# Graph attention on one core: the adjacency mask kept as -1 and the step function as 127 or infinity

## What is computed

```python
seq    = (x @ W_seq).reshape(N, H, DH)              # N = 2048, D = 512, H = 16, DH = 32
score1 = einsum('nhd,d->hn', seq, a1)
score2 = einsum('nhd,d->hn', seq, a2)
scores = leaky_relu(score1[:, :, None] + score2[:, None, :], 0.2)
attn   = softmax(scores + (1 - adj) * -65500, axis=-1)
hidden = einsum('hij,jhd->ihd', attn, seq).reshape(N, D)
x      = layernorm(x + elu(hidden @ W_out + b_out))
# second layer: dinv = (1 + row sums of (adj + adj.T) / 2) ** -0.5
x      = layernorm(x + adj @ (dinv * (((adj + adj.T) / 2 + I) @ (dinv * x))))
```

## Time and profile before

| what | value |
|---|---|
| median of 3 executions | 741.42 us (740.29 to 742.1) |
| profiled execution, its own time | 740.72 us |
| its span in the trace | 738.9 us |
| granted TensorE clock, mean | 0.998 of full speed |
| busy: PE, DVE, ACT, POOL | 98%, 71%, 55%, 16% of the span |
| prologue, up to the first attention matmul | about 67.6 us |
| attention stage | 67.6 to 447 us |
| all after it | 447 to 738.9 us |

### The profile page before, as it was taken

One profiled execution on the slowest core, in us unless ns is written; L12 is line 12 of the kernel. 1 busy time (PEld: TensorE's weight loads), 2 busy tenths in 40 slices (PEclk: granted clock), 3 DMA queues, 4 the chain that ended last, 5 costly groups with the idle time before them and its releaser, 6 DMA issues.

```text
span 738.9 us, 23474 instructions
## 1 busy us (share of the span) xinstructions
PE 722.7 (98%) x10731; PEld 560.0 (76%) x10731; DVE 526.6 (71%) x885; ACT 409.6 (55%) x315; POOL 117.6 (16%) x145
## 2 busy tenths in 40 slices
PE   7999899999999999999999999999999999999996
PEld 5878899999999999999999995444444444444444
DVE  4568999999999999999999984877830110332332
ACT  1678998888988998898988952333220110000000
POOL 0200110001221212213000002655312100000000
PEclk9999999999999999999999999999999999999999
DMA  9994315213532344333221122994059500101101
GB/s 334 417 419 162 110 54 149 61 46 74 88 63 64 61 82 83 63 65 59 59 59 36 47 82 50 184 188 101 23 87 170 85 1 1 41 31 43 43 29 43
DMA packets 33351, 71.24 MB, mean 96 GB/s; under 512 B 3044, under 2 KB 14052, under 8 KB 31076
## 3 DMA queue, kind: packets, MB, share of 16 engines
q1 hardware_dynamic: 24736, 51.64, 20.3%
q0 software_dynamic: 8240, 17.84, 17.0%
q10 hardware_dynamic: 276, 0.26, 0.1%
HBM read 77.86 MB, written 8.65 MB: 117 GB/s over the span
## 4 chain that ended last, share of the span: by engine, by line
PE 81%; DVE 8%; issue 5%; DMA 4%; SPq 1%; POOL 1%; ACT 0%; POOLq 0%; DVEq 0%; ACTq 0%
PE bank L635 20%; PE bank L742 14%; PE bank L636 12%; PE bank L728 11%; PE bank L691 8%; PE bank L641 4%; PE bank L699 4%; PE bank L640 4%; PE bank L639 4%; DVE RZ L1081 3%; DMA RZ<-in_L_gnn_W_seq_dram 2%; DVE RG L1095 1%; DMA RZ<-s_rows_dram 1%; DVE RG L1091 1%; SPq L345 1%
## 5 line engine op out<-in xcount | busy, mean ns | idle before, releaser
L635 PE MATMUL bank<-RP,RG 128*128 128x132 f16 (+1 forms) x3072 | 375.3, 220 | 2.8 <-DVE RG L1091 1.5
L636 PE MATMUL bank<-RP,MT 128*128 128x66 f16 (+1 forms) x3072 | 375.0, 196 | 0.0
L820 ACT ACTIVATE RZ<-RZ,TAB 128x2048 int8<-128x2048 f32 x159 | 305.0, 1994 | 24.8 <-DVE RG L1091 22.1
L635 PEld LDWEIGHTS bank<-RP,RG 128*128 128x128 fp8e4 x3072 | 284.8, 98 | 3.7 <-DVE RG L1091 1.8
L636 PEld LDWEIGHTS bank<-RP,MT 128*128 128x128 fp8e4 x3072 | 284.7, 97 | 0.0
L640 PE MATMUL bank<-RP,RG 128*128 128x66 f16 (+1 forms) x1024 | 199.2, 194 | 0.0
L641 PE MATMUL bank<-RP,MT 128*128 128x66 f16 (+1 forms) x1024 | 198.9, 194 | 0.0
L639 PE MATMUL bank<-RP,RG 128*128 128x66 f16 (+1 forms) x1024 | 198.0, 193 | 0.0
L1081 DVE TENSOR_SCALAR RZ<-RZ,TAB 128x2048 int8<-128x2048 f32 x97 | 123.0, 1268 | 2.3 <-DMA RZ<-s_rows_dram 2.2
L742 PE MATMUL bank<-RZ,MT 128*128 128x512 f16 (+1 forms) x544 | 110.8, 366 | 0.0
L1091 DVE TENSOR_TENSOR RG<-RZ,MT 128x512 int32<-128x512 int32 x159 | 107.7, 677 | 0.0
(11 more groups left out here) (138 smaller groups left out, 724.1 us busy)
## 6 DMA issues: line engine op xcount, KB each, us to landing
RG<-in_adj_t_dram SPq DMA_DIRECT2D x16, 1024.0 KB, 8.1
RZ<-s_rows_dram SPq DMA_DIRECT2D x60, 256.0 KB, 3.3
seq_copy_dram<-SEQ SPq DMA_DIRECT2D x8, 528.0 KB, 5.4
RZ<-in_x_dram SPq DMA_DIRECT2D x16, 256.0 KB, 3.0
RP<-in_adj_p_dram POOLq DMA_DIRECT2D x8, 512.0 KB, 8.2
RP<-in_adj_tp_dram POOLq DMA_DIRECT2D x8, 512.0 KB, 12.4
out_dram<-W SPq DMA_DIRECT2D x16, 256.0 KB, 2.0
RQ<-in_x_t_dram SPq DMA_DIRECT2D x2, 1024.0 KB, 14.3
```

The costliest lines, as they stand in the source:

```text
L635: mm(bank[:, c:c + 4 * d], step, both, start=(j == 0 and i % IB == 0), **ends)
L636: last = mm(bank[:, c:c + 4 * d].rearrange("p (e c d) -> p e c d", e=2, c=2)[:, :, 1, :], mask, pn[:, 4:6, :], start=False, **ends)
L820: A(Z[:, m % NZ, :], S1B[u], ACT.Sign, bias=S2[:, h, j:j + 1], scale=-1.0).then_inc(z_ready, 1)
```

## The change

The mask MT is kept as -1 in float8 (the cast gets the scale -1). A raw step is the byte 127 on DVE, and on ACT infinity in float8, from a rectifier whose argument is s1 + s2 times 2^40; a new table SK holds S2 times 2^40. Both bytes, anded with the byte of -1, give the byte of +1. So G is +1 as before, and the mask product is now negative. The operands are four slots: high E, high F, low E, low F. The step product takes all four; the mask product takes slots 1 and 3, two runs of 33 with 33 between, and gives G F minus adj F. The final sum becomes a difference. The negation L1009 goes. Slots 0 and 1 are written by ACT, slots 2 and 3 by DVE, each as one run of 66 per tile. The operands of a tile take 264 bytes a partition and not 396, so that TN, TB, ND, V2 and VMT move down in RP. Where the mask is used elsewhere, signs follow (degrees, column sums, -1/ZS at the end).

```diff
-        Z = RZ[:, 0:2048].bitcast(i8).rearrange("p (s n) -> p s n", s=NZ)
+        Z8 = RZ[:, 0:2048].bitcast(f8).rearrange("p (s n) -> p s n", s=NZ)
...
-        PNW = NT * 6 * (DV + 1) // 2
+        PNW = NT * 4 * (DV + 1) // 2
...
-            return RP[:, o:o + NT * 3 * w].bitcast(f16).rearrange("p (t c d) -> p t c d", t=NT, c=6)
+            return RP[:, o:o + NT * 2 * w].bitcast(f16).rearrange("p (t c d) -> p t c d", t=NT, c=4)
...
+                own.mark(gp.tensor_scalar(SK[:, hs], S2[:, hs], STEEP, 1.0, ALU.mult, ALU.mult))
                 own.mark(gp.tensor_scalar(S2[:, hs], S2[:, hs], -1.0, 1.0, ALU.mult, ALU.mult))
...
-                    high, low, edge = (pn[:, c:c + 2, :].rearrange("p c d -> p (c d)") for c in (0, 2, 4))
-                    both = pn[:, 0:4, :].rearrange("p c d -> p (c d)")
+                    high, low = (pn[:, c:c + 2, :].rearrange("p c d -> p (c d)") for c in (0, 2))
+                    both, edge = pn.rearrange("p c d -> p (c d)"), pn[:, 1:4:2, :]
...
-                                      pn[:, 4:6, :], start=False, **ends)
+                                      edge, start=False, **ends)
...
-                            last = mm(bank[:, c + d:c + 3 * d], mask, edge, start=False, **ends)
+                            last = mm(bank[:, c + d:c + 3 * d].rearrange("p (c d) -> p c d", c=2), mask, edge, start=False, **ends)
...
-                A(MT8[:, t, :], adj_f[:, t % NA, :], ACT.Copy, saturate=False, accum_out=CS[:, t:t + 1]).then_inc(adj_cast, 1)
+                A(MT8[:, t, :], adj_f[:, t % NA, :], ACT.Copy, scale=-1.0, saturate=False, accum_out=CS[:, t:t + 1]).then_inc(adj_cast, 1)
...
-                A(operands(h)[:, :, 0:5:4, 0:DV], V2[:, :, :, :], ACT.Copy).then_inc(hi_ready, 1)
+                A(operands(h)[:, :, 0:2, 0:DV], V2[:, :, :, :], ACT.Copy).then_inc(hi_ready, 1)
...
-                A(Z[:, m % NZ, :], S1B[u], ACT.Sign, bias=S2[:, h, j:j + 1], scale=-1.0).then_inc(z_ready, 1)
+                A(Z8[:, m % NZ, :], S1B[u], ACT.Relu, bias=SK[:, h, j:j + 1], scale=STEEP, saturate=False).then_inc(z_ready, 1)
...
+                    own.mark(V.tensor_scalar(half(e, SK), half(e, S2), STEEP, None, ALU.mult))
                     own.mark(V.tensor_scalar(half(e, S2), half(e, S2), -1.0, None, ALU.mult))
...
-                    own.mark(V.memset(pn[:, :, 4, DV], 1.0))
-                own.mark(V.tensor_tensor(pn[:, :, 2:6:3, 0:DV], V2[:, :, :, :], pn[:, :, 0:5:4, 0:DV], ALU.subtract))
-                own.wait(ve)
-                V.tensor_scalar(pn[:, :, 1:4:2, 0:DV], pn[:, :, 4:6, 0:DV], -1.0, None, ALU.mult).then_inc(pn_ready, 1)
+                    own.mark(V.memset(pn[:, :, 0:2, DV], 1.0))
+                    own.wait(ve)
+                V.tensor_tensor(pn[:, :, 2:4, 0:DV], V2[:, :, :, :], pn[:, :, 0:2, 0:DV], ALU.subtract).then_inc(pn_ready, 1)
...
-                at = (DV + 1) + DV
-                V.tensor_copy(r[:, :, 0:IB - 1], wide(h, 0)[:, :, :, at]).then_inc(row_sb, 1)
-                V.tensor_copy(r[:, :, IB - 1], narrow(h, 1, 2)[:, :, DV]).then_inc(row_sb, 1)
+                ones_e, ones_f = DV, (DV + 1) + DV
+                own.mark(V.tensor_copy(r[:, :, 0:IB - 1], wide(h, 0)[:, :, :, ones_e]))
+                own.mark(V.tensor_copy(r[:, :, IB - 1], narrow(h, 0, 1)[:, :, DV]))
+                own.wait(ve)
+                V.tensor_tensor(r[:, :, 0:IB - 1], r[:, :, 0:IB - 1], wide(h, 0)[:, :, :, ones_f], ALU.subtract).then_inc(row_sb, 1)
+                V.tensor_tensor(r[:, :, IB - 1], r[:, :, IB - 1], narrow(h, 1, 2)[:, :, DV], ALU.subtract).then_inc(row_sb, 1)
...
-                own.mark(V.scalar_tensor_tensor(ND, TN[:, :, 0, :], TINY, ND, ALU.add, ALU.add))
+                own.mark(V.scalar_tensor_tensor(ND, TN[:, :, 0, :], TINY, ND, ALU.add, ALU.subtract))
...
-                V.tensor_scalar(ZD[:, m % 2, :], S1B[u], S2[:, h, j:j + 1], -1.0, ALU.is_gt, ALU.mult).then_inc(zd_ready, 1)
+                V.tensor_scalar(ZD[:, m % 2, :], S1B[u], S2[:, h, j:j + 1], STEP, ALU.is_gt, ALU.mult).then_inc(zd_ready, 1)
```

More of the change, by code:

```diff
@@ L37, in gat_then_normalised_adjacency @@
     TINY = 1e-30
+    STEP = 127.0
+    STEEP = 2.0 ** 40
     TOP = 2.0 ** 15
@@ L154, in gat_then_normalised_adjacency @@
         ones = sb("ones", [P, P], bf16)
-        TAB = sb("TAB", [P, 5, H, NT], f32)
-        S1, S2, EE, FF, RHO = (TAB[:, i] for i in range(5))
+        TAB = sb("TAB", [P, 6, H, NT], f32)
+        S1, S2, EE, FF, RHO, SK = (TAB[:, i] for i in range(6))
         VC = sb("VC", [P, 3, H], f32)
@@ L1036, in lone_nodes @@
                 own.mark(V.tensor_scalar(LONE[:, :], ROW[:, :], 0.0, None, ALU.is_equal))
-                own.mark(V.tensor_tensor(DINV[:, :], ROW[:, :], CS[:, :], ALU.add))
+                own.mark(V.tensor_tensor(DINV[:, :], ROW[:, :], CS[:, :], ALU.subtract))
                 own.wait(ve)
@@ L1289, in sum_tile @@
                     ve.wait_ge(out_st[u], (t // 2) * 16)
-                V.scalar_tensor_tensor(yw[:, u, :], pb[(t + NQ) % 8][:, :], 1.0 / ZS, X1[:, t, 0:D],
+                V.scalar_tensor_tensor(yw[:, u, :], pb[(t + NQ) % 8][:, :], -1.0 / ZS, X1[:, t, 0:D],
                                        ALU.mult, ALU.add).then_inc(ov_done, 1)
@@ L1301, in last_half @@
                     ve.wait_ge(out_st[u], (t // 2) * 16)
-                V.scalar_tensor_tensor(yw[:, u, cols], pb[(t + NQ + e) % 8][:, cols], 1.0 / ZS, X1[:, t, cols],
+                V.scalar_tensor_tensor(yw[:, u, cols], pb[(t + NQ + e) % 8][:, cols], -1.0 / ZS, X1[:, t, cols],
                                        ALU.mult, ALU.add).then_inc(ov_done, 1)
```

## The result

| | before | changed |
|---|---|---|
| median | 741.76 us (4 runs) | 734.08 us (4 runs) |
| ratio | | 0.9897 (0.9877 to 0.9916) |
| profiled execution, span | 740.72, 738.9 us | 734.38, 732.6 us |
| matmuls between 90 and 400 us | 7614 | 7742 |

The forecast was 742.7 us with a chance of 0.14 for faster. The time is within about 1 us of the rival called faster, 735.1. The clock did nothing: granted 1.00 in both in the stretch from 90 to 400 us.

What follows compares the result with a forecast made beforehand. PE was taken to bound the attention stage, DVE only its start and a gap in head 7. Terms -0.4 - 0.3 + 2.0 = +1.3 us gave 742.7 us, own range 740.5 to 744, low end 735, high end 753.

Steps and rivals of the forecast that it cites:

- the rival called faster: PE's edge matmuls all cost as the aligned one: -5.6 us, with -0.7 from DVE, 735.1 us; chance 0.14.
- What bounds the kernel: Attention stage: PE sets the pace, DVE barely keeps up and bounds only the stage's start and a head 7 gap.
- The negation, 0.5 us a head: DVE's L1009, once a head: removal frees 8 us over 16 heads, off the path wherever PE sets the pace.
- The start: Chain over DVE before tile 5 of head 0: without L1009 everything behind it moves up, -0.4 us.
- The gap in head 7, -0.3: PE's wait for a late mask, 254.66 to 255.01 us: vanishes as DVE gets ahead, -0.3 us.
- Does a start address matter, +2.0 us: PE's edge matmuls: a start on 16 bytes saves 1.9 ns; none stays aligned, so 68 tiles lose 0.03 us each.
- The break in the run, 0: Edge operand read as two runs of 66 bytes: taken as 0, upper end 102 us at half read speed.
- Both slower rivals: Edge operands: second run costs as off-16-byte start, 750.5 us, chance 0.24; paired reading lost, 755 to 845 us, chance 0.12.
- Steps, table, cast, SK, degrees: 0: Steps on ACT and DVE, ACT table loads, adjacency cast, table SK, head 3's degree subtractions: no added time, 0.

## Why the prediction was wrong

- **What bounds the kernel**: right that PE sets the pace where DVE keeps up, and that DVE barely does. I did not put a number on "barely". Had I taken DVE's heads as I took PE's tiles, I would have found 23.5 against 23.43 us.
- **The negation, 0.5 us a head**: its size was right (DVE's plain heads 23.23 to 22.76). Its worth was mis-stated, because I had it as hidden work wherever PE sets the pace. Left out alone, from head 3 on, it took away the waits in head 7 (that head of PE fell from 23.86 to 23.43 us), and the time fell by 0.3 to 1.8 us (740.38 against 741.07). But with PE's operands moved it is worth 4 to 7 us: 739.91 to 735.78, and 740.87 to 734.08 or 734.58.
- **The start**: tile 5 of head 0 began at 77.81 instead of 78.07 us although the S1 row landed 0.20 us later (61.61), so -0.46, near the -0.4 forecast. The first matmul did not come earlier, 67.72 after 67.63.
- **The gap in head 7, -0.3**: came in part. PE lost 0.32 us before tile 13 and 0.10 before tile 12, which I had overlooked; now it loses 0.20 before tile 13. PE became as much faster as DVE, so DVE's masks were hardly further ahead (0.47 us at the head's start, 0.26 before).
- **Does a start address matter, +2.0 us**: this is the step that failed. The rows' period of four was real and so was its link to 16 bytes. The reason I gave (a start off 16 bytes costs) was wrong, and the trace could not tell it from the right one: in the fast tiles the edge starts on 16 bytes and, being adjacent, the slots end there too. From the wrong one it followed that no edge would be fast; from the right one that all are. The term measured (360.0 - 366.1) x 1024 groups = -6.2 us instead of +2.0. The faster rival had these 1.9 ns an edge and the sign, and no mechanism; it got the least chance but one for that. That its 735.1 came so near is in part luck: it added -5.6 for PE and -0.7 for DVE as if each could be had alone, and PE's part alone gave 1.0 us.
- **The break in the run, 0**: right. Edges of two runs take 30.0 ns, and the run with the edge cut at bytes 264 and 344 shows no cost of the cut. Both slower rivals fall with it. The Trainium skill (Advanced Engine Details and Errata, section "SBUF Cachelines") says that an access to a different line of 16 bytes is penalised, and that two hits on a line are enough to avoid it. No run here shows such a penalty for one line more: the edge touches ten lines now for nine and is faster. That does not refute the section, as all of these lines are read for two or more numbers, save one of the ten in every second tile. The size of the line agrees with the period in the trace.
- **Steps, table, cast, SK, degrees: 0**: right. ACT's step takes 1.994 us as rectifier into eight-bit float as it did as sign into int8, with one table load, and PE waits for no mask in heads 1 to 6, so nothing of the rest reached it. The Trainium skill (ScalarE: Activation LUTs, section "Table sets: the hidden batching unit"), by which a rectifier needs no other set, is borne out by that load.

## What to carry to other kernels

When two engines are both busy 99% of a stage, work out each one's time per repetition from its own starts. If the two agree, as here, a saving on either may be worth next to nothing until the other has one too, and the experiment is the two-by-two of both. And when a period in the trace fits an address rule, list what else has that period (here the end of the read before, as well as the start of this one) before the rule is carried over to a new layout.

## What the runs showed of the hardware that I had not expected

A matmul of 66 columns behind one of 132 starts its successor after 29 to 30 ns, but after 33 to 34 ns if its moving operand begins in the same 16 bytes in which the operand before it ended (byte 264 or 268 behind 263; not 276 or 66, nor the byte right behind the end where that is a multiple of 16, as in one tile in four before: 29.2). The four slots before it are then somewhat quicker (57 against 58 to 60 ns). The net cost sits in the three edges behind four slots alone: from byte 268 to byte 276 the group's first six matmuls went from 272.6 to 264.2 ns, 2.8 for each of these edges, and the last three took 95.9 in both. From the kernel before to the changed one it was 270.9 to 264.6, 2.1 each, and 95.1 to 95.4. Among three short matmuls in a row one took 36 ns in the changed kernel, and which one moved with the layout (the second at byte 132, the third at byte 144, none at byte 148, where the next long one took 61.6 ns). The cause of that was not found.
